# Attention and mixture of experts on one core: value products two tiles of keys at a time

## The reference

```
h = x + Attention(layernorm(x))       # 32 query heads of 16, 8 key/value heads (each used by 4 query heads)
    scores = Q K^T / sqrt(16);  attn = softmax(scores);  out = attn V;  out @ Wo + bo
y = h + MoE(layernorm(h))             # 8 experts, the best 2 for each token, softmax of the two logits
    expert output = t @ expert_w[e]^T + expert_b[e]
```

## Time and profile before

| | |
|---|---|
| median of three runs | 1973.47 us |
| profiled execution, its span | 1974.0 us |
| TensorE (PE) busy | 1827.0 us, 93% |
| VectorE (DVE) busy | 1436.3 us, 73% |
| ScalarE (ACT) busy | 1203.5 us, 61% |
| attention, first to last exponential | about 141 to 1627 us |

### The profile page before, as it was taken

One profiled execution on the slowest core, in us unless ns is written; L12 is line 12 of the kernel. 1 busy time (PEld: TensorE's weight loads), 2 busy tenths in 40 slices (PEclk: granted clock), 3 DMA queues, 4 the chain that ended last, 5 costly groups with the idle time before them and its releaser, 6 DMA issues.

```text
span 1974.0 us, 35320 instructions
## 1 busy us (share of the span) xinstructions
PE 1827.0 (93%) x9850; PEld 684.5 (35%) x9851; DVE 1436.3 (73%) x1599; ACT 1203.5 (61%) x2291; POOL 204.3 (10%) x220
## 2 busy tenths in 40 slices
PE   6997999999999999999999999999999988857980
PEld 3532333333333333333333333333333216625870
DVE  4495888888888888888888888888888705562214
ACT  2334777777777777777777777777777783322330
POOL 4443120000000000000000000000000004051006
PEclk9998999999999999999999999999999998967995
DMA  5226330100100000001000100100000004034548
GB/s 180 82 74 113 130 113 18 33 11 14 32 11 11 11 32 11 11 11 32 11 11 18 33 11 14 32 3 3 3 24 3 25 4 151 1 133 149 165 138 255
DMA packets 77019, 104.49 MB, mean 53 GB/s; under 512 B 28072, under 2 KB 49592, under 8 KB 76992
## 3 DMA queue, kind: packets, MB, share of 16 engines
q1 hardware_dynamic: 62624, 61.37, 10.8%
q0 software_dynamic: 11920, 40.93, 6.0%
q10 hardware_dynamic: 2448, 1.84, 0.4%
HBM read 58.49 MB, written 45.22 MB: 53 GB/s over the span
## 4 chain that ended last, share of the span: by engine, by line
PE 87%; DVE 3%; POOL 3%; DMA 2%; issue 2%; ACT 1%; ACTq 0%; SPq 0%; DVEq 0%; POOLq 0%
PE bank L805 25%; PE bank L773 24%; PE bank L799 22%; PE bank L902 7%; PE bank L744 3%; DVE max_kc L1093 2%; DMA arena_q<-q_parts 1%; POOL slots_x L411 1%; PE bank L817 1%; PE bank L979 1%; POOL ys L420 1%; POOL xs L420 1%; PE bank L759 1%; ACT arena_p L639 1%; PE bank L929 1%
## 5 line engine op out<-in xcount | busy, mean ns | idle before, releaser
L1093 DVE TENSOR_REDUCE max_kc<-bank 128x1 f32<-128x1024 f32 x1024 | 1212.0, 1219 | 207.7 <-PE bank L773 201.2
L639 ACT ACTIVATE arena_p<-bank 128x512 f32<-128x512 f32 x2048 | 1057.5, 603 | 406.3 <-PE bank L799 402.4
L799 PE MATMUL bank<-arena_q,arena_k 99*128 (+1 forms) x2048 | 617.2, 379 | 22.1 <-DMA arena_q<-q_parts 14.0
L773 PE MATMUL bank<-arena_k,arena_q 96*128 (+1 forms) x2048 | 614.7, 381 | 3.4 <-DVE max_kc L1093 3.1
L805 PE MATMUL bank<-arena_p,v_cur 128*32 128x512 f32 x4096 | 546.0, 605 | 0.7 <-ACT arena_p L639 0.7
L773 PEld LDWEIGHTS bank<-arena_k,arena_q 96*128 (+1 forms) x2048 | 161.7, 97 | 501.4 <-issue 337.9
L799 PEld LDWEIGHTS bank<-arena_q,arena_k 99*128 (+1 forms) x2048 | 196.7, 97 | 394.0 <-ACT arena_p L639 159.4
L805 PEld LDWEIGHTS bank<-arena_p,v_cur 128*32 128x32 f32 x4096 | 80.6, 108 | 125.2 <-issue 109.9
L353 POOL COPY v_cur<-v_all 128x256 f32 (+1 forms) x8 | 3.2, 399 | 1159.3 <-PE bank L805 1159.2
L1245 DVE TENSOR_TENSOR x2T_lo<-bank,x2T_hi 128x512 fp32r<-128x512 f32 x39 | 27.0, 692 | 106.0 <-ACT x2T_hi L646 106.0
L744 PE MATMUL bank<-xT,arena_p 128*128 128x512 f32 x160 | 75.6, 594 | 2.8 <-ACT xT L587 2.8
(11 more groups left out here) (153 smaller groups left out, 883.0 us busy)
## 6 DMA issues: line engine op xcount, KB each, us to landing
arena_q<-q_parts SPq DMA_DIRECT2D x192, 64.0 KB, 2.3
slots_x<-be_sb POOLq DMA_DIRECT2D x39, 256.0 KB, 2.3
xs<-slots_x SPq DMA_DIRECT2D x39, 256.0 KB, 2.7
slots_y<-ys SPq DMA_DIRECT2D x39, 256.0 KB, 2.0
we_raw<-in_L_ffn_expert_w POOLq DMA_DIRECT2D x8, 1024.0 KB, 6.1
q_parts<-arena_k SPq DMA_DIRECT2D x16, 384.0 KB, 3.0
heads_out<-o_norm SPq DMA_DIRECT2D x33, 128.0 KB, 2.3
at<-heads_out SPq DMA_DIRECT2D x4, 1024.0 KB, 6.6
```

The lines of the kernel that those rows point to most:

```text
L639: act.activation(probs[:, u % PRING, :], bank[:, ring_bank(("score", u)), :], ACT.Exp, scale=SCALE).then_inc(p_ready, 1)
L773: mm = pe.matmul(bank[:, 2 + 2 * (m % 2) + q, :], q_flat[0:CROW, bass.ds(qo, P)], k_flat[0:CROW, bass.ds((j // NC) * T + (2 * half + q) * ...
L799: pe.matmul(bank[:, ring_bank(("score", u)), :], k_flat[0:SROW, bass.ds((i // NC) * T + kt * P, P)], q_flat[0:SROW, bass.ds(qo, CH)], star ...
L1093: dve.reduce_max(max_kc[:, m:m + 1], bank[:, 2 + 2 * (m % 2):4 + 2 * (m % 2), :].rearrange("p a s -> p (a s)"), AX.X).then_inc(m_done, 1)
```

## The change

Where step kt had the value product of tile kt-1, now only the even steps have products: step 2, 4, ..., 14 those of tiles kt-2 and kt-1, one directly after the other, and step 0 those of tiles 14 and 15 of the round before. The odd steps have none. The waits for `v_ready` and `o_ready` go from step 1 to step 2 with the first product. After the last round the products of tiles 14 and 15 follow. Nothing else is changed: number and form of all instructions stay.

```diff
@@ attention_step
                 score_unit(i, REP * kt + 2)
-                if kt >= 1:
-                    if kt == 1:
+                if kt >= 2 and kt % 2 == 0:
+                    if kt == 2:
                         pe.wait_ge(v_ready, i // NC + 1)
                         pe.wait_ge(o_ready, i + 1)
+                    value_product(i, kt - 2)
                     value_product(i, kt - 1)
-                elif not (isinstance(i, int) and i == 0):
+                elif kt == 0 and not (isinstance(i, int) and i == 0):
+                    value_product(i - 1, NKT - 2)
                     value_product(i - 1, NKT - 1)
                 if kt == 2:
                     output_transpose(i)
@@ after the last round
             other_steps(N - 1)
+            value_product(N - 1, NKT - 2)
             value_product(N - 1, NKT - 1)
             output_transpose(N)
```

## The result

The changed kernel takes 2026.18 us (median of four runs, 2024.09 to 2027.56), the kernel before 1974.88. The ratio is 1.0257, with a 95% interval of 1.0241 to 1.0272: slower by 51 us. The forecast was 2026, within 2008 to 2050.

The account below looks back on a forecast made before the run. TensorE was taken to set the pace. 29 rounds at +1.62 us gave +47.0; with +0.6, +0.6, +5.0 and -0.4 that made +52.8 on 1974.0, less 0.5: 2026 us, range 2008 to 2050 (chance 0.83).

Parts of the forecast that it names:

- 2 to 4: Steps where output transposes delay VectorE's work and its reduction comes late: +0.13 us per round.
- 8 to 10: Steps where VectorE's max_q comes between reductions: 0.28 more waiting and 0.11 for a transpose, 6.24 against 5.77, +0.47.
- 10 to 12: Steps where small shift operations push VectorE's reductions by up to 0.3: slack just holds, +0.18.
- TensorE alone: Two steps without any wait: 5.47 us against 5.67, so -0.20 per pair, from one exit and one entry saved.
- The join of the two products: Between two adjacent value products on TensorE: taken as 0.45 us, with bounds 0.43 and 0.64.
- The three score banks: ScalarE hands banks back late between two pairs of products: 0.38 us new waiting, 5.85 instead of 5.67, +0.18 per regular pair.
- two steps without maxima: The last 11 pairs, held by ScalarE's exponentials: 5.24 us instead of 2 x 2.39, +0.45 each, +5.0 in all.
- regular pair: Two ordinary steps with maxima, no extra VectorE work between: 5.85 us instead of 5.67, +0.18.
- VectorE: Reductions handing back two pairs of maximum banks: 0.13 us slack, no cost regularly; cost where other VectorE work lies between.
- its two ends: Outside the 29 full rounds: +0.6 in round 0, +0.6 in round 30, +5.0 without maxima, -0.4 at the end.
- Waits forecast at nothing: Moved waits for v_ready and o_ready, the probabilities' places, POOL's copy of v_cur and SyncE's queue: 0 each.
- The copy of bank 6: On ScalarE in steps 0 to 2, in the pause the products leave: costs nothing, 0.5 us if the pause were gone.

Follow-up runs that it names:

- E3: The changed kernel with each exponential over half its columns and each maximum over half its keys: 1900.4 us, ratio 0.9632 to the kernel before.
- E7: The changed kernel with the second maximum unit put between the two products of an even step, so they are not adjacent: 2070.41 us, ratio 1.0486.
- E1: The changed kernel with each exponential over 256 of its 512 columns: 2001.51 us, ratio 1.0145 to the kernel before.
- E2: The changed kernel with each maximum taken over 512 instead of 1024 keys: 1998.67 us, ratio 1.0128 to the kernel before.
- E9: The changed kernel with six score banks in the last round only and that round's products one step later, still in pairs: 2010.86 us, ratio 1.0185.
- E4: The kernel before, products singly, with exponentials over half the columns and maxima over half the keys: 1961.42 us, ratio 0.9935.
- E8: The kernel before, products singly, with six score banks in the last round only and that round's products one step later: 1965.02 us, ratio 0.9954.
- E6: The changed kernel with one pair per round undone, tiles 8 and 9 singly in steps 9 and 10: 2007.23 us, ratio 1.0172.

## Why the prediction was right

By its steps, as forecast and measured, in us per pair of steps:

| steps | forecast | measured | before |
|---|---|---|---|
| 0 to 2 | 6.34 | 6.30 | 6.23 |
| 2 to 4 | 6.00 | 6.04 | 5.87 |
| 4 to 6, 6 to 8, 12 to 14 | 5.85 | 5.81 | 5.67 |
| 8 to 10 | 6.24 | 6.29 | 5.77 |
| 10 to 12 | 5.85 | 5.87 | 5.67 |
| 14 to 0 | 5.91 | 5.89 | 5.72 |
| a round | 47.89 | 47.80 | 46.27 |

- **TensorE alone.** Forecast -0.20 per pair (5.47). With nobody late it is 5.43, thus -0.23 (E3). The join of the two products costs no more than a pass inside one: the four passes take 1.86, not 1.89. That term was mis-sized by 0.03 per pair, some 8 us in all; steps 2 to 4 and 8 to 10 went against it by 0.04 and 0.05. The Trainium skill, TensorEngine Tiling (Array Packing), Key Properties, has it that a change of tiling mode drains TensorE. E3 and E7 agree: one way out and in less is worth 0.23 and 0.24. At the same places the type changes from bf16 to f32 and back, and no run separates the two.
- **The three score banks.** Forecast 2.54 from s3 to the second next s1, measured 2.54; for two steps without maxima forecast 5.24, measured 5.21. That it decides in a regular pair, and not TensorE or VectorE, is shown by E1, E2 and E3 together, and in steps without maxima by E9. But the forecast put the whole 0.38 of new waiting there. In the trace 0.18 of it comes earlier, at Mb of the odd step, which waits for VectorE; the VectorE paragraph doesn't ask about this unit. ScalarE's wait comes later and takes up what is left, so the sum was right all the same.
- **VectorE.** Forecast: no cost in a regular pair with 0.13 of slack, 0.28 in steps 8 to 10. E2 shows that regular pairs lose nothing to it. Their slack was smaller, 0.07, since VectorE's chain gives 5.74 (E1) and ScalarE's 5.81. Steps 8 to 10 lose 6.29 - 5.91 = 0.38, within the bounds but not 0.28; steps 2 to 4 lose 0.23 where 6.00 - 5.85 = 0.15 was forecast, and steps 10 to 12 lose 0.06 where the slack was to hold. The Trainium skill, TensorEngine Tiling (Array Packing), PSUM Bottleneck, says that a faster TensorE may find the emptying of PSUM in its way. That holds here in a sharper form: there was time enough on average (ScalarE idles 1.78 in 5.81), but not between two pairs.
- **Sum.** Forecast +52.8 for the profiled execution, measured 2024.3 - 1974.0 = +50.3. Of these 29 rounds at 1.53 make 44.4. Attention as a whole, from the first copy of bank 6 to the last, went from 1485.3 to 1536.2, +50.9, so 6.5 is left for its two ends, forecast 5.8.
- **Waits forecast at nothing** (probabilities' ring, v_ready, copy of v_cur, SyncE): no pair of steps is longer than its forecast by more than 0.05. The copy of bank 6 stays in the pause (1.14 idle before it at 733.59).

That the time came out as 2026.18 for a forecast of 2026 is luck. The runs of the changed kernel alone lie between 2024.09 and 2027.56, and the steps' errors, VectorE's share too small and the regular pairs 0.04 too long, cancel within a round to 0.09. The mechanism isn't luck: its loop of three banks gave the steps without maxima to 0.01 us before anything was changed.

## What to carry to other kernels

When work on the limiting engine is bunched to save a switch, draw the chain of hand-backs for the stretch between two bunches: start of an exponential after its score, so many intervals, its length, the return. If it is longer than the engine's own work there, the saving is lost and more, however much the helpers idle on average. Test that chain first on a stretch of the old trace where it already binds (here the steps without maxima): it gave that step to 0.01 us. Draw it for every unit and every engine that hands a buffer back, also for those that seem to have time: VectorE's wait of 0.18 was found only in the trace. And where two chains are nearly equal, take away each alone and both together: alone they took 0.07 and nothing off a regular pair, together 0.38 (25, 27 and 126 us of the kernel, of which 6 us in the second and third lie ahead of attention).

## What the runs showed of the hardware

- Two f32 products on four column strips of the array directly after one another join without a gap: 16 matmuls in 1.86 us up to the next bf16 matmul, against 0.99 for 8. Going into and out of such a stretch from bf16 matmuls cost 0.23 to 0.24 (E3, E7).
- The granted clock right after attention differed from kernel to kernel, though the same phase follows. In two stretches of 6 us, from 0.6 us after the start of the last copy of bank 6, it was 0.71 and 0.72 in the kernel before, 0.72 and 0.71 in E1 and in E4, 0.83 and 0.88 in E8, 0.88 and 0.84 in E6, and 1.00 in the changed kernel, E2, E3 and E9 (1.00 is 2.4 GHz, 0.5 is 1.2 GHz; what lies between is a mean of the two). It doesn't follow pairs or single products: E1 has pairs and the clock of the kernel before. In the changed kernel it fell later, to 0.72 from 1704.5 to 1710.5. What decides it the runs don't show, and each kernel was profiled once. So a few us behind a changed stage shouldn't be put down to the edit.
